# Attention outputs moved from a transpose bank to the two-bank ring, with eleven fillers fewer

## The chip, the cores and the metric

The kernel runs on one core of one Trainium2 chip. The metric is the device time of one execution in microseconds; lower is better. The time before is the median of three runs. The profile comes from one execution, whose own time stands beside its span.

## The reference

A gated block over `x` of 8 batches x 100 tokens x 512. First a cross-attention to a context of 8 x 361 x 256 (16 query heads, 8 key heads of 128), then a transformer layer whose self-attention and mixture of experts are what follows here:

```
h = rms(layernorm(x)) * w_ln1
q, k, v = h @ wq + bq, h @ wk + bk, h @ wv + bv      # 16 heads of 32
q, k = rope(q, k)
attn = softmax(causal(q k^T / sqrt(32)))             # 100 x 100 per head and batch
x = x + (attn @ v) @ wo
h = rms(x) * w_ln2;  top-2 of 8 experts (352 wide) + a shared expert (1408 wide)
```

All of it is in fp32 quality. The large products are done as three matmuls on a high and a low part of each operand (`mm3`).

## The kernel before, in words

Each engine runs its own list of instructions in order, and semaphores tie them together. One list of steps, `steps_ffn`, sets the order of the second half of the kernel for all engines; each engine picks its part out of each step.

The 8 batches are in two halves of 4. Self-attention is the step `("at", n)`, n from 0 to 35. A unit u (0 to 31) is four heads of one batch: batch u // 4. The four heads of a unit have one bank of scores (banks 0, 1, 2, 5) and one tile `PF`. The way of a unit goes over several steps:

- PE: `f_scores(q, pair)`, the scores of two units of batch q, two steps or more ahead ("scores q").
- DVE: `f_max`, the row extremum; ACT: four exponentials into `PF`; DVE: reciprocal, and the scaling multiplication (from unit 22 on POOL does the multiplication, L1993).
- PE at step u + 3: "turn u", four transposes of `PF` into bank 3 (even u) or bank 4 (odd u), L2413. ACT copies the even ones to `PTf`, DVE the odd ones (L1593).
- PE at step 4q + 7: "out q", `f_out(q)`, 16 small products of batch q, into bank 4 in the kernel before. ACT copies the bank to `CXh` (the high part, L1132), and DVE subtracts to get `CXl` (the low part, event `dve_cx`).

On ACT and DVE the work of step n is done in this order: the copy of the transposed unit, then CXh or CXl, then the exponentials (ACT), or the scaling and the next row extremum (DVE).

Between the steps stand other products of PE. They take two banks in turn, 6 and 7, which is called the ring here. `Plan.banks` walks through the list of steps and gives each user the next bank of the two and, as its wait, the event with which the previous user of that bank was emptied. `free_bank` waits for it. Users of the ring, in order: `qk` 0 to 7 of the second half (query and key products), `vbat` 0 to 3 (value products of the second half; DVE's addition `("vadd", i)` of the bias, L1574, empties the bank), `po` 0 to 3 (output projection), `er` 0 to 3, `eh` 0 to 3 (transposes, with DVE work on the rows between them), `elog`, `gate` 0, `esoft` (LT transposes, L2462), `up` 0, and the second half's `po`. In the list, `("at", 15)` (with out 2) stands between `vbat` 1 and `vbat` 2, and `("vadd", 1)` right behind `("at", 15)`. `("at", 35)` (with out 7) is followed by `esoft` 0 and `up` 0. After step `moe1` the ring has all eight banks.

Fillers are products of the identity with itself, whose results nobody reads (`keep_warm`). Each shows in the trace as two matmul records. `WARM` places some in front of named work. `WARM_RING` places others, and gives with the number the user of the ring in whose bank they are written; so a group of fillers also waits for that bank.

`mm` (L2074) is the helper that issues most matmuls, so this line stands for many kinds of work; the tiles tell them apart. L1357 is the same for DVE's subtractions (low parts).

Of the kernel before, what the change touches and what calls it, by code (L numbers as in the profile page):

```python
# [21 lines left out]
FH, FD = 16, 32  # L22
# [30 lines left out]
WARM = {"head": 12, ("x_turn", 0, 1): 3, ("q", 0, 0): 4, "swap": 4, "vrow": 7, "scores": 4, ("turn", 3): 2, ("po", 0, 0): 3,  # L53
        ("elog", 0): 3}

WARM_RING = {("scores", 2, 0): (4, ("qk", 1, 5)), ("turn", 9): (3, ("vbat", 0)), ("scores", 5, 0): (5, ("po", 0, 0)),
             ("turn", 21): (3, ("er", 0, 1)), ("scores", 7, 0): (2, ("er", 0, 3)), ("out", 5): (3, ("eh", 0, 0)),
             ("turn", 25): (6, ("eh", 0, 0)), ("out", 6): (3, ("eh", 0, 3)), ("turn", 29): (2, ("elog", 0)),
             ("out", 7): (4, ("esoft", 0))}

AHEAD = {"x": 3, "f": 4, "e": 4}
SLOTS = {"x": 4, "f": 6, "e": 6}
# [291 lines left out]
class Plan:  # L354
# [86 lines left out]
    def banks(self):  # L441

        empty = {6: ("dve_x1", 7), 7: ("dve_x1", 8)}
        self.bank, self.bank_free = {}, {}
        count, n, ring = {}, 0, [6, 7]

        def signal(name):
            count[name] = count.get(name, 0) + 1
            return name, count[name]

        def use(key, gone):
            nonlocal n
            bank = ring[n % len(ring)]
            self.bank[key], self.bank_free[key] = bank, empty[bank]
            empty[bank] = gone
            n += 1

        for s in self.ffn:
            if s[:2] == ("qk", 1):
                use(s, ("act_f", 8 - len(BY_PE) + s[2] + 1))  # L460
            elif s[0] == "vbat":
                use(s, ("dve_v", HB + s[1] + 1))
            elif s[0] == "po":
                use(s, ("act_ytf", s[1] * KD + s[2] + 1))
            elif s[0] == "er":
                use(s, ("dve_x2", s[1] * HB + s[2] + 1))
            elif s[0] == "eh":
                use(s, ("dve_h2", s[1] * HB + s[2] + 1))
            elif s[0] == "elog":
                use(s, ("act_lt", s[1] + 1))  # L470
            elif s[0] == "esoft":
                use(s, ("dve_l", s[1] + 1))
            elif s[0] == "moe1":
                empty |= {0: ("act_fe", 32), 1: ("act_fe", 32), 2: ("act_fe", 32), 5: ("act_fe", 32), 3: ("act_ft", 16), 4: ("dve_cx", 8)}
                n, ring = 0, list(range(8))
            elif s[0] == "gate":
                gone = signal("act_th")
                use(s, gone if s[2] else signal("dve_silu"))
            elif s[0] == "up":
                use(s, signal("dve_gu"))  # L480
            elif s[0] == "down" and s[3] == 0:
                use(s[:3], ("act_y", s[1] * KD + s[2] + 1))
            elif s[0] == "rank":
                use(s, ("dve_route", ROUTE["pos"]))
            elif s[0] == "inverse":
                use(s, ("dve_meta", 3))
            elif s[0] == "xt":
                use(s, ("dve_xe", s[1] + 1))
            elif s[0] == "eg":
                use(s, ("act_et", s[1] + 1))  # L490
            elif s[0] == "eu":
                use(s, ("dve_em", s[1] + 1))
            elif s[0] == "ea":
                use(s, ("dve_ea", s[1] + 1))
            elif s[0] == "ed":
                use(s, ("act_ey", s[1] + 1))
            elif s[0] == "srow":
                use(s, ("dve_sr", s[1] * HB + s[2] + 1))
# [15 lines left out]
def flamingo_kernel(nc, x, ctx_in, mask, g_x, g_f, Wq, Wk, Wv, Wo, w_ln1, wq, b_q, wk, b_k, wv, b_v, wo,  # L514
# [6 lines left out]
    def sem(name):  # L521
        if name not in handles:
            handles[name] = top.enter_context(nc.semaphore(name))
        return handles[name]
# [367 lines left out]
    def scalar_program(eng):  # L892
# [227 lines left out]
        def self_attention(n):  # L1120
            u = n - 3
            if 0 <= u < 32 and u % 2 == 0:
                act.wait_ge(sem("pe_ft"), u + 1)
                if u >= 6:
                    act.wait_ge(sem("pe_fo"), (u - 6) // 4 + 1)
                eng.activation(flat(PTf[u % 6][:, :, :]), banks[3 + u % 2][0:T, 0:4 * T], ACT.Copy).then_inc(sem("act_ft"), 1)
            u = n - 4
            if u >= 0 and u % 4 == 3:
                h, b = divmod(u // 4, HB)
                act.wait_ge(sem("pe_fo"), u // 4 + 1)  # L1130
                src = banks[4][:, 0:4 * T].rearrange("p (a b) -> p a b", a=4)
                eng.activation(CXh[h][:, :, batch_slice(b)], src, ACT.Copy).then_inc(sem("act_cx"), 1)  # L1132
            u = n
            if u < 32:
                act.wait_ge(sem("dve_fn"), u + 1)
                if u >= 4:
                    act.wait_ge(sem("pe_ft"), u - 3)
                p, m, bank = PF[u % 4], sm[u % 4], score_bank[u % 4]
                for c in range(4):
                    e = eng.activation(p[:, c, :], bank[0:T, c * T:(c + 1) * T], ACT.Exp, bias=m[:, 1, c:c + 1],  # L1140
                                       scale=-1.0, accum_out=m[:, 2, c:c + 1])
                e.then_inc(sem("act_fe"), 1)
# [199 lines left out]
    def vector_program(eng):  # L1342
# [242 lines left out]
        def self_attention(n):  # L1585
            if n == 0:
                f_max(0)
            u = n - 3
            if 0 <= u < 32 and u % 2:
                dve.wait_ge(sem("pe_ft"), u + 1)  # L1590
                if u >= 6:
                    dve.wait_ge(sem("pe_fo"), (u - 6) // 4 + 1)
                eng.tensor_copy(flat(PTf[u % 6][:, :, :]), banks[3 + u % 2][0:T, 0:4 * T]).then_inc(sem("dve_ft"), 1)  # L1593
            u = n - 4
            if u >= 0 and u % 4 == 3:
                h, b = divmod(u // 4, HB)
                dve.wait_ge(sem("act_cx"), u // 4 + 1)
                src = banks[4][:, 0:4 * T].rearrange("p (a b) -> p a b", a=4)
                low(CXl[h][:, :, batch_slice(b)], src, CXh[h][:, :, batch_slice(b)]).then_inc(sem("dve_cx"), 1)
            u = n - 1  # L1600
            if 0 <= u < 32:
                p, m = PF[u % 4], sm[u % 4]
                dve.wait_ge(sem("act_fe"), u + 1)
                if u in BY_POOL:
                    eng.reciprocal(m[:, 3, :], m[:, 2, :]).then_inc(sem("dve_frec"), 1)
                else:
                    chained(eng.reciprocal(m[:, 3, :], m[:, 2, :]))
                    r4 = m[:, 3, :].rearrange("p (a o) -> p a o", o=1).broadcast_to([T, 4, T])
                    eng.tensor_tensor(p[:, :, :], p[:, :, :], r4, ALU.mult).then_inc(sem("dve_fp"), 1)
            if n + 1 < 32:  # L1610
                f_max(n + 1)
# [457 lines left out]
    def tensor_program(eng):  # L2069
# [3 lines left out]
        def mm(o, a, b, start, stop):  # L2073
            return eng.matmul(o, a, b, start=start, stop=stop, skip_group_check=True)  # L2074
# [303 lines left out]
        def f_out(q):  # L2378

            h, b = divmod(q, HB)  # L2380
            warm_ring("out", q)
            pe.wait_ge(sem("act_ft"), 2 * q + 2)
            pe.wait_ge(sem("dve_ft"), 2 * q + 2)
            pe.wait_ge(sem("dve_v"), HB * (h + 1))
            if q:
                pe.wait_ge(sem("dve_cx"), q)
            else:
                pe.wait_ge(sem("dve_ht"), B - 1)
            for c in range(4):
                for i in range(4):  # L2390
                    at = (4 * c + i) * FD
                    e = mm(banks[4][32 * i:32 * i + 32, c * T:(c + 1) * T], V[h][:, b, at:at + FD],
                           PTf[(4 * q + i) % 6][:, c, :], True, True)
            e.then_inc(sem("pe_fo"), 1)

        def self_attention(n):
            u = n - 3
            if 0 <= u < 32:
                warm_ring("turn", u)
                if u < 2:  # L2400
                    pe.wait_ge(sem("dve_v"), HB)
                    pe.wait_ge(sem("dve_ht"), B - 1)
                elif u % 2 == 0:
                    pe.wait_ge(sem("act_ft"), u // 2)
                else:
                    pe.wait_ge(sem("dve_ft"), u // 2)
                    if u >= 5:
                        pe.wait_ge(sem("dve_cx"), (u - 5) // 4 + 1)
                keep_warm(banks[3 + u % 2], WARM.get(("turn", u), 0))
                name, value = plan.scaled(u)  # L2410
                pe.wait_ge(sem(name), value)
                for c in range(4):
                    e = eng.transpose(banks[3 + u % 2][0:T, c * T:(c + 1) * T], PF[u % 4][:, c, :], ident[0:T, 0:T])  # L2413
                e.then_inc(sem("pe_ft"), 1)
# [276 lines left out]
```

## Time and profile before

| | |
|---|---|
| median of 3 runs | 929.7 us (928.98 to 931.67) |
| profiled execution | 929.81 us, span 928.0 us |
| PE busy | 901.6 us (97%) |
| PE weight load busy | 842.2 us (91%) |
| DVE busy | 634.6 us (68%) |
| ACT busy | 559.1 us (60%) |
| POOL busy | 323.9 us (35%) |
| mean granted TensorE clock | 0.996 |
| chain that ended last | PE 61%, DVE 17%, DMA 12% |
| self-attention stage | about 507 to 617 us of the span |

Busy times are sums over the whole span. The chain is followed back from the last instruction, at each step to what released it. The self-attention stage is where the change is; its rows stand two sections below. A matmul row's time is that of a merged piece, start first, then duration.

### The profile page before, as it was taken

The page shows a single profiled execution, that of the slowest core. Times are in us where ns is not written, and L with a number is a line of the kernel's source. Part 1 is how long each engine was busy: PE and PEld are TensorE (multiplying, and loading weights), DVE is VectorE, ACT ScalarE, POOL GpSimd, SP SyncE. Part 2 cuts the span into 40 slices and gives each one's busy share as a digit, 9 for nine tenths or more (in the row PEclk, how much of TensorE's full clock was granted, in tenths as well). Part 3 has the DMA queues.
Part 4 walks back from the last instruction along what each step waited for, and adds up shares of the span by engine and source line. Part 5 has one row for each costly group of instructions (what it writes and reads, how often), then busy time and mean ns, then how long its engine had stood idle before and what let it go on. Part 6 is the DMA issues. An engine that isn't in the chain of part 4 may idle for free.

```text
span 928.0 us, 16511 instructions
## 1 busy us (share of the span) xinstructions
PE 901.6 (97%) x5905; PEld 842.2 (91%) x5905; DVE 634.6 (68%) x1482; ACT 559.1 (60%) x1448; POOL 323.9 (35%) x344
## 2 busy tenths in 40 slices
PE   8999999999999999999999999899999999999996
PEld 8889999999999999999987877689999999999996
DVE  3657777664446777673286985857585989898864
ACT  3666766663555666674432766745436787778851
POOL 3532323335552223234643542334401232323211
PEclk9999999999999999999999999999999999999999
DMA  5733720006450000002542111114438899999975
GB/s 158 217 93 109 202 82 2 7 18 173 141 160 23 17 1 1 2 12 58 157 117 85 58 51 54 48 59 116 115 93 291 291 328 319 332 303 328 298 193 153
DMA packets 112761, 122.22 MB, mean 132 GB/s; under 512 B 9887, under 2 KB 77927, under 8 KB 112680
## 3 DMA queue, kind: packets, MB, share of 16 engines
q1 hardware_dynamic: 97806, 98.80, 34.0%
q0 software_dynamic: 5184, 12.13, 5.8%
q10 hardware_dynamic: 9690, 10.24, 3.8%
q8 instruction: 47, 0.77, 0.3%
q14 instruction: 34, 0.28, 0.1%
HBM read 110.72 MB, written 19.07 MB: 140 GB/s over the span
## 4 chain that ended last, share of the span: by engine, by line
PE 61%; DVE 17%; DMA 12%; issue 4%; ACT 4%; POOL 1%; ACTq 0%; SPq 0%; DVEq 0%; POOLq 0%
PE bank L2074 55%; DMA eraw<-in_L_ffn_w_gate_e_dram 8%; PE bank L2223 4%; DVE we L1357 2%; DVE wf L1357 2%; ACT we L930 1%; DMA raw<-in_L_xattn_Wq_dram 1%; DMA sums<-s_sum 1%; DVE TE L1782 1%; DVE sm L1583 1%; DMA raw<-s_unit 1%; DMA X<-in_x_dram 1%; DVE HDl L1357 1%; DVE PQ L1559 1%; DVE TM L1767 1%
## 5 line engine op out<-in xcount | busy, mean ns | idle before, releaser
L1943 POOL TENSOR_SCALAR SC<-SC,mx,anyv 100x361 f32<-100x361 f32 x128 | 81.7, 650 | 210.1 <-DVE mx L1468 199.2
L1357 DVE TENSOR_TENSOR we<-eraw,we 128x704 fp32r<-128x704 f32 (+2 forms) x140 | 107.4, 798 | 25.2 <-ACT we L930 25.0
L930 ACT ACTIVATE we<-eraw 128x704 fp32r<-128x704 f32 (+2 forms) x140 | 96.7, 719 | 39.4 <-DMA eraw<-in_L_ffn_w_gate_e_dram 22.4
L1926 POOL TENSOR_TENSOR wx<-raw,wx 128x512 fp32r<-128x512 f32 x64 | 83.5, 1314 | 72.4 <-ACT wx L916 72.3
L1926 POOL TENSOR_TENSOR wf<-raw,wf 128x512 fp32r<-128x512 f32 x54 | 71.7, 1334 | 103.4 <-ACT wf L916 103.4
L2074 PE MATMUL bank<-H2h,wf 128*128 128x400 f32 x352 | 100.2, 351 | 0.0
L1046 ACT ACTIVATE SC<-SC,mx 100x361 f32<-100x361 f32 x128 | 75.4, 593 | 29.1 <-DVE mx L1464 28.3
L1357 DVE TENSOR_TENSOR Kl<-bank,Kh 128x362 fp32r<-128x362 f32 x64 | 34.0, 534 | 58.8 <-ACT Kh L1004 58.8
L1357 DVE TENSOR_TENSOR QOl<-bank,QOh 128x200 fp32r<-128x200 f32 (+1 forms) x96 | 41.4, 432 | 45.6 <-ACT QOh L959 35.5
L2074 PE MATMUL bank<-XTh,wx 128*128 128x400 f32 x256 | 70.8, 351 | 0.5 <-POOL wx L1926 0.5
L2004 POOL DMA_INDIRECT XB<-s_h,inv x20 | 22.2, 1108 | 140.5 <-PE bank L2520 116.8
L916 ACT ACTIVATE wf<-raw 128x512 fp32r<-128x512 f32 x100 | 61.6, 628 | 15.7 <-DMA raw<-s_unit 7.6
L2074 PE MATMUL bank<-QOh,wx 128*128 128x400 f32 x256 | 70.8, 347 | 0.0
L2074 PEld LDWEIGHTS bank<-H2h,wf 128*128 128x128 f32 x352 | 65.7, 189 | 0.1
L1461 DVE CUSTOM_DVE_ANT_0 SC<-bank,mb 100x361 f32<-100x361 f32 x128 | 62.6, 527 | 0.3
L1037 ACT ACTIVATE PTh<-bank 128x400 fp32r<-128x400 f32 x64 | 32.4, 506 | 50.1 <-PE bank L2223 49.9
L2074 PE MATMUL bank<-H2l,wf 128*128 128x400 f32 x176 | 60.7, 345 | 0.0
L1357 DVE TENSOR_TENSOR PTl<-bank,PTh 128x400 fp32r<-128x400 f32 (+1 forms) x128 | 53.2, 457 | 7.5 <-ACT PTh L1037 7.5
L916 ACT ACTIVATE wx<-raw 128x512 fp32r<-128x512 f32 x64 | 40.0, 627 | 26.7 <-PE bank L2074 8.9
L2074 PE MATMUL bank<-PTl,Vh 128*128 128x200 f32 (+1 forms) x192 | 52.8, 275 | 0.0
L2074 PE MATMUL bank<-PTh,Vl 128*128 128x200 f32 (+1 forms) x192 | 52.7, 275 | 0.0
L2074 PE MATMUL bank<-PTh,Vh 128*128 128x200 f32 (+1 forms) x192 | 52.0, 271 | 0.0
(291 smaller groups left out, 2730.6 us busy)
## 6 DMA issues: line engine op xcount, KB each, us to landing
raw<-s_unit SPq DMA_DIRECT2D x60, 256.0 KB, 3.1
eraw<-in_L_ffn_w_gate_e_dram SPq DMA_DIRECT2D x40, 352.0 KB, 4.5
eraw<-in_L_ffn_w_up_e_dram SPq DMA_DIRECT2D x40, 352.0 KB, 5.1
eraw<-in_L_ffn_w_down_e_dram SPq DMA_DIRECT2D x40, 256.0 KB, 5.4
raw<-in_L_xattn_Wq_dram SPq DMA_DIRECT2D x32, 256.0 KB, 3.2
raw<-in_L_xattn_Wo_dram SPq DMA_DIRECT2D x32, 256.0 KB, 2.9
eraw<-in_L_ffn_w_down_e_dram SPq DMA_DIRECT2D x20, 192.0 KB, 5.0
s_unit<-in_L_ffn_w_sh_gate_dram SPq DMA_DIRECT2D x11, 256.0 KB, 3.6
```

Source lines behind the costliest of these rows:

```text
L916: eng.activation(weights(stream, u)[:, 0, :, :], raw[r % 4][:, :, :], ACT.Copy).then_inc(sem("act_w"), 1)
L930: eng.activation(weights("e", u)[0:rows, 0, 0:n], eraw[u % 6][0:rows, 0:n], ACT.Copy).then_inc(sem("act_e"), 1)
L1037: eng.activation(flat(PTh[t % 2][:, 0:2, :]), banks[5][:, 0:4 * T], ACT.Copy).then_inc(sem("act_pt"), 1)
L1046: eng.activation(sc, sc, ACT.Exp, bias=mx[t % 3][:, 1, h:h + 1], scale=XS, accum_out=mx[t % 3][:, 2, h:h + 1]).then_inc(sem("act_exp"), 1)
L1357: return eng.tensor_tensor(o, src, f32(hi), ALU.subtract)
L1461: eng.tensor_tensor_reduce(SC[t % 3][:, h, :], banks[h][0:T, 0:S], mb[:, :], 1.0, -3.0e38, ALU.add, ALU.max, m[:, 0, h:h + 1]).then_inc(se ...
L1559: chained(eng.tensor_tensor(by_batch(p[:, 1, :]), by_batch(p[:, 1, :]), sin4, ALU.mult))
L1926: eng.tensor_tensor(w[:, 1, :, :], raw[plan.raw[stream, u] % 4][:, :, :], f32(w[:, 0, :, :]), ALU.subtract).then_inc(sem("pool_w"), 1)
L1943: eng.tensor_scalar(sc, sc, m[:, 3, h:h + 1], anyv[:, b:b + 1], ALU.mult, ALU.mult).then_inc(sem("pool_p"), 1)
L2004: eng.indirect_dma_start(XB[i % 2][:, :], None, s_h2, bass.IndirectOffsetOnAxis(ap=inv[:, i:i + 1], axis=0)).then_inc(sem(f"dma_xb{i % 2}" ...
L2074: return eng.matmul(o, a, b, start=start, stop=stop, skip_group_check=True)
L2223: e = eng.transpose(dst, SC[t % 3][:, h, o:o + n], ident[0:T, 0:T])
```

## The change

The outputs of self-attention become users of the ring: each takes the next of banks 6 and 7 when its step comes. ACT and DVE read them from there. PE's odd transposes lose their wait for `dve_cx`. The ring's later users move on by one place at every output. After `moe1`, bank 4 waits for the last copy of an odd transpose instead of for the last `CXl`. The filler groups before turn 9 (3), turn 21 (3) and turn 29 (2) go, that before turn 25 has 3 instead of 6, and the others are written into other users' banks.

```diff
--- before.py
+++ after.py
@@ -53,10 +53,8 @@
 WARM = {"head": 12, ("x_turn", 0, 1): 3, ("q", 0, 0): 4, "swap": 4, "vrow": 7, "scores": 4, ("turn", 3): 2, ("po", 0, 0): 3,
         ("elog", 0): 3}
 
-WARM_RING = {("scores", 2, 0): (4, ("qk", 1, 5)), ("turn", 9): (3, ("vbat", 0)), ("scores", 5, 0): (5, ("po", 0, 0)),
-             ("turn", 21): (3, ("er", 0, 1)), ("scores", 7, 0): (2, ("er", 0, 3)), ("out", 5): (3, ("eh", 0, 0)),
-             ("turn", 25): (6, ("eh", 0, 0)), ("out", 6): (3, ("eh", 0, 3)), ("turn", 29): (2, ("elog", 0)),
-             ("out", 7): (4, ("esoft", 0))}
+WARM_RING = {("scores", 2, 0): (4, ("out", 0)), ("scores", 5, 0): (5, ("out", 3)), ("scores", 7, 0): (2, ("er", 0, 3)),
+             ("out", 5): (3, ("out", 5)), ("turn", 25): (3, ("eh", 0, 0)), ("out", 6): (3, ("out", 6)), ("out", 7): (4, ("out", 7))}
 
 AHEAD = {"x": 3, "f": 4, "e": 4}
 SLOTS = {"x": 4, "f": 6, "e": 6}
@@ -460,6 +458,8 @@
                 use(s, ("act_f", 8 - len(BY_PE) + s[2] + 1))
             elif s[0] == "vbat":
                 use(s, ("dve_v", HB + s[1] + 1))
+            elif s[0] == "at" and s[1] >= 7 and s[1] % 4 == 3:
+                use(("out", s[1] // 4 - 1), ("dve_cx", s[1] // 4))
             elif s[0] == "po":
                 use(s, ("act_ytf", s[1] * KD + s[2] + 1))
             elif s[0] == "er":
@@ -471,7 +471,7 @@
             elif s[0] == "esoft":
                 use(s, ("dve_l", s[1] + 1))
             elif s[0] == "moe1":
-                empty |= {0: ("act_fe", 32), 1: ("act_fe", 32), 2: ("act_fe", 32), 5: ("act_fe", 32), 3: ("act_ft", 16), 4: ("dve_cx", 8)}
+                empty |= {0: ("act_fe", 32), 1: ("act_fe", 32), 2: ("act_fe", 32), 5: ("act_fe", 32), 3: ("act_ft", 16), 4: ("dve_ft", 16)}
                 n, ring = 0, list(range(8))
             elif s[0] == "gate":
                 gone = signal("act_th")
@@ -1128,7 +1128,7 @@
             if u >= 0 and u % 4 == 3:
                 h, b = divmod(u // 4, HB)
                 act.wait_ge(sem("pe_fo"), u // 4 + 1)
-                src = banks[4][:, 0:4 * T].rearrange("p (a b) -> p a b", a=4)
+                src = banks[plan.bank["out", u // 4]][:, 0:4 * T].rearrange("p (a b) -> p a b", a=4)
                 eng.activation(CXh[h][:, :, batch_slice(b)], src, ACT.Copy).then_inc(sem("act_cx"), 1)
             u = n
             if u < 32:
@@ -1595,7 +1595,7 @@
             if u >= 0 and u % 4 == 3:
                 h, b = divmod(u // 4, HB)
                 dve.wait_ge(sem("act_cx"), u // 4 + 1)
-                src = banks[4][:, 0:4 * T].rearrange("p (a b) -> p a b", a=4)
+                src = banks[plan.bank["out", u // 4]][:, 0:4 * T].rearrange("p (a b) -> p a b", a=4)
                 low(CXl[h][:, :, batch_slice(b)], src, CXh[h][:, :, batch_slice(b)]).then_inc(sem("dve_cx"), 1)
             u = n - 1
             if 0 <= u < 32:
@@ -2382,14 +2382,11 @@
             pe.wait_ge(sem("act_ft"), 2 * q + 2)
             pe.wait_ge(sem("dve_ft"), 2 * q + 2)
             pe.wait_ge(sem("dve_v"), HB * (h + 1))
-            if q:
-                pe.wait_ge(sem("dve_cx"), q)
-            else:
-                pe.wait_ge(sem("dve_ht"), B - 1)
+            bank = free_bank(("out", q))
             for c in range(4):
                 for i in range(4):
                     at = (4 * c + i) * FD
-                    e = mm(banks[4][32 * i:32 * i + 32, c * T:(c + 1) * T], V[h][:, b, at:at + FD],
+                    e = mm(bank[32 * i:32 * i + 32, c * T:(c + 1) * T], V[h][:, b, at:at + FD],
                            PTf[(4 * q + i) % 6][:, c, :], True, True)
             e.then_inc(sem("pe_fo"), 1)
 
@@ -2404,8 +2401,6 @@
                     pe.wait_ge(sem("act_ft"), u // 2)
                 else:
                     pe.wait_ge(sem("dve_ft"), u // 2)
-                    if u >= 5:
-                        pe.wait_ge(sem("dve_cx"), (u - 5) // 4 + 1)
                 keep_warm(banks[3 + u % 2], WARM.get(("turn", u), 0))
                 name, value = plan.scaled(u)
                 pe.wait_ge(sem(name), value)
```

## Rows read from the trace of the kernel before

**Rows 1.** Busy time of each engine in four stretches: busy (count) for each, clock, DMA share, GB/s.

```profile
511.00:550.90 39.90, 37.54 (x345) 31.77 (x343) 37.85 (x76) 29.60 (x130) 20.79 (x16) 1.00 0.18 54
550.90:584.80 33.90, 33.03 (x328) 27.09 (x329) 18.19 (x42) 21.43 (x93) 10.76 (x8) 1.00 0.21 62
584.80:604.50 19.70, 16.40 (x180) 12.92 (x182) 19.28 (x45) 14.71 (x74) 6.83 (x8) 0.97 0.12 36
604.50:617.00 12.50, 11.57 (x128) 10.15 (x128) 2.86 (x8) 5.85 (x16) 2.99 (x3) 0.91 0.12 39
```

**Rows 2.** The chain that ended last, around 550 us: start, us, what.

```profile
550.25 0.58 DVE KT L1562
550.87 4.37 PE bank L2074 x30
```

**Rows 3.** Who PE waited for, 660 to 928 us, longest: us, times, longest.

```profile
PE bank L2074 <- DVE we L1357: 1.1, 2, 0.6
```

**Rows 4.** Who PE waited for, 505 to 660 us.

```profile
PE bank L2413 <- DVE CXl L1357: 1.8, 3, 1.0
```

**Rows 5.** PE in order of time: start, us, instruction, [idle before]; turns 5, 6, fillers, turn 10.

```profile
534.09 0.55 PE L2413 MATMUL bank<-ident,PF 100*100 100x100 f32 x4 [1.04 <-DVE CXl L1357]
535.79 0.55 PE L2413 MATMUL bank<-ident,PF 100*100 100x100 f32 x4
544.27 0.83 PE L2074 MATMUL bank<-ident 128*128 128x128 f32 x6
547.17 0.55 PE L2413 MATMUL bank<-ident,PF 100*100 100x100 f32 x4
```

**Rows 6.** Two scalings on DVE, POOL beside the first, all 22 (ns min/median/max).

```profile
534.15 1.40 DVE L1609 TENSOR_TENSOR PF<-PF,sm 100x400 f32<-100x400 f32 x1
545.53 1.40 DVE L1609 TENSOR_TENSOR PF<-PF,sm 100x400 f32<-100x400 f32 x1
533.84 1.28 POOL L1926 TENSOR_TENSOR wf<-raw,wf 128x512 fp32r<-128x512 f32 x1 [2.96 <-ACT wf L916]
L1609 DVE TENSOR_TENSOR PF<-PF,sm x22: 574/574/1477, 511.3 to 580.1; 100x400 f32<-100x400 f32 x22
```

**Rows 7.** ACT and PE in order of time, around turn 21.

```profile
585.84 0.23 ACT L1140 ACTIVATION_READ_ACCUMULATOR PF<-bank,sm 100x1 f32 x1
586.12 0.54 PE L2074 MATMUL bank<-causb,identb 100*100 100x400 bf16 x2
```

**Rows 8.** PE and DVE around out 2 and vbat 2.

```profile
555.51 0.89 PE L2074 MATMUL bank<-PTf,V 100*32 100x100 f32 x32
556.34 0.71 PE L2074 MATMUL bank<-wf,HTh 128*100 128x512 f32 x2
557.01 0.57 DVE L1357 TENSOR_TENSOR CXl<-bank,CXh 128x400 fp32r<-128x400 f32 x1 [2.76 <-ACT CXh L1132]
558.68 0.68 DVE L1574 TENSOR_TENSOR V<-bank,bvb 100x512 f32<-100x512 f32 x1
```

**Rows 9.** DVE's CXl of out 3, and the product of PE that waited for it.

```profile
569.43 0.57 DVE L1357 TENSOR_TENSOR CXl<-bank,CXh 128x400 fp32r<-128x400 f32 x1 [2.08 <-ACT CXh L1132]
570.15 0.42 PE L2074 MATMUL bank<-CXh,wf 128*128 128x400 f32 x1 [0.46 <-DVE CXl L1357]
```

**Rows 10.** PE, ACT and DVE around up 0.

```profile
616.72 0.45 PE L2074 MATMUL bank<-H2h,wf 128*128 128x400 f32 x1
616.56 0.50 ACT L1132 ACTIVATE CXh<-bank 128x400 fp32r<-128x400 f32 x1 [1.90 <-PE bank L2074]
617.09 0.57 DVE L1357 TENSOR_TENSOR CXl<-bank,CXh 128x400 fp32r<-128x400 f32 x1 [1.63 <-ACT CXh L1132]
```

**Rows 11.** Stretches around 603 us, columns as in rows 1, and out 6 on PE.

```profile
600.00:603.00 3.00, 1.61 (x12) 1.07 (x12) 3.00 (x7) 2.94 (x18) 0.85 (x1) 1.00 0.46 135
603.40:603.60 0.20, 0.20 (x3) 0.20 (x2) 0.20 (x3) 0.20 (x1) 0.00 (x0) 0.50 0.35 133
604.43 1.56 PE L2074 MATMUL bank<-PTf,V 100*32 100x100 f32 x32
```

## The prediction

> **What bounds the kernel now.** I read the page first: PE is busy 97% of the span, and the chain that ended last is 61% PE. That average says nothing about the stretch which the change edits, so I read stage by stage. The table of stretches [rows 1] splits the self-attention stage (511 to 617 us) by engine. From 511.0 to 550.9 DVE is busy 37.85 of 39.9 us while PE, with its fillers, still leaves 2.4 us idle; from 584.8 to 604.5 DVE is busy 19.28 of 19.7 us and PE only 16.4. Between them, 550.9 to 584.8, PE is busy 33.03 of 33.9 and DVE 18.19. The chain of waits says the same: it runs on DVE up to the addition that ends the rotary embedding at 550.83, and goes over to PE at 550.87 [rows 2], where the scores of batch 4 wait for that addition. So there are two parts where DVE sets the pace and one between them where PE does. After 617 us PE is the pace again: its whole list of waits from 660 us on has three lines, the largest 1.1 us [rows 3]. A delay of PE that is not made good by 617 us therefore reaches the end, and so does a gain.
>
> **What the change removes.** It takes the attention outputs ("out q") off bank 4, so the odd transposes ("turn u") need not wait for the subtraction that reads that bank (CXl), and drops 11 fillers. Waits of PE's transposes for CXl: 1.8 us over three [rows 4]. Fillers: three took 0.83 us [rows 5], so 0.28 each, and 11 take 3.0 us. At most 4.8 us in all. How much lies on the path?
>
> Turn 5, 1.04 us idle before 534.09 [rows 5]. Without it PE does turn 5 and scores 2 about 1.0 us sooner, and then stands at turn 6. Turn 6 needs the scaling of its tile, a DVE multiplication that ran 534.15 to 535.55 [rows 6]; PE started turn 6 at 535.79 [rows 5]. So at most 0.2 us is left of the 1.04. The same at turn 9: 0.83 of fillers and 0.37 of waiting go, turn 10 needs a multiplication that ran 545.53 to 546.93 and started itself at 547.17 [rows 5, 6], again 0.2 left. The scores of batch 4 then wait for the addition at 550.83 whatever PE did before [rows 2], and DVE had no gap that PE could close. Gain of both: 0. Bounds: 0 and the 2.2 us that stood there.
>
> Turn 21 (three fillers): next comes the second half of scores 6, started at 586.12, which needs an exponential that ACT ended at 586.07 [rows 7]. ACT does it behind the copy of out 4. Gain 0, with PE idle there instead. Turn 25 (six fillers become three, and a wait of 0.40): PE comes to the next transposes of the router rows (eh) 0.2 to 0.4 us sooner, but turn 27 after those waits for POOL, which waits for DVE, full in this part [rows 1]. Gain 0. Turn 29 (two fillers): the router's product after it waits for the low part of the last H2 tile, which hangs on ACT's queue behind out 6. Gain 0. What is left of the edit is PE idle in place of fillers.
>
> Here the Trainium skill bears on the DVE parts. The trace shows the scaling multiplication of turn 6 at 1.40 us while POOL ran a product from 533.84 to 535.12, while the median of all 22 is 0.57 [rows 6]. GPSIMD Engine Reference, Specifications: GpSimd shares its SBUF interfaces with VectorE and collides with VectorE instructions that have two SBUF inputs. By that rule each pair that meets or parts is worth about 0.8 us either way on the DVE path, and the sum would be 0.8 more or less.
> By the rows no POOL product moves here, since each starts behind an ACT operation that starts behind DVE, and the term is 0.
>
> **What it adds.** "Out q" takes its turn in the ring of banks 6 and 7, so every later user of the ring moves by one place at each out. I went through the ring user by user: bank, the event that frees it, and when that event stood in this trace. Nearly all stay covered (the nearest are the products that now need the CXl of an out: qk 6 for out 0, where turn 5, which waited for that same CXl, stands 2 us before it; and in the same way vbat 0, er 1 and eh 1, each behind a turn that waited for that CXl). Two do not.
>
> *First stall: vbat 2.* The order is vbat 0 (bank 6), vbat 1 (bank 7), out 2 (bank 6), vbat 2 (bank 7). So vbat 2 now waits for the bias addition that empties vbat 1; before, for that of vbat 0, long done. On DVE this addition is queued behind step 15, and step 15 holds CXl of out 2, which waits for ACT's copy of out 2, which waits for PE's out 2: the product right before vbat 2. The trace has the whole chain: out 2 is over at 556.34 and vbat 2 starts at once; ACT copies; DVE's CXl, which had waited 2.76 us for that copy, starts at 557.01, then a reciprocal, a multiplication and a maximum, and the addition runs 558.68 to 559.36 [rows 8]. From a DVE end to PE's start is 0.15 us (570.00 to 570.15) [rows 9]. So vbat 2 starts at 559.51 and not 556.34: 3.17 us. This is in the PE part; behind it turn 13, scores, vbat 3, turns 14 and 15 follow on PE, and ACT's exponential that scores 5 waits for stands behind turn 14. All move. Bounds: 0, if the addition came earlier, and 3.2.
>
> *Second stall: up 0.* Near the end gate and up of the first hidden tile also use the ring. Up 0 had the bank of gate 0; now it has that of out 7, so it waits for the CXl of out 7. Between the two PE has only four small transposes. Up 0 started at 616.72; ACT's copy began at 616.56, and CXl ran 617.09 to 617.66 [rows 10]. With 0.15 for the release up 0 starts at 617.81: 1.09 us. The output product that comes after needs this CXl anyway, but PE did all of up 0 before it, so nothing makes this good. Bounds 0 and 1.1.
>
> **The clock.** The granted clock is 1.00 almost everywhere, but 0.50 around 603.4 to 606.6 (the 1.2 of the two levels, 1.2 and 2.4 GHz), after 600 to 603 in which PE was busy 1.61 of 3.0 us [rows 11]. The low stretch was about 3.4 us long, and PE's work in it took nearly twice: out 6 1.56 us, out 2 0.89 [rows 8, 11]. The first stall leaves PE without any work for 3.17 us, less than in that stretch, so I expect a low stretch there too, at a place where PE sets the pace. If all 3.4 us of it fall on work they cost 1.7 us; part will fall on the idle time itself. Bounds 0 and 1.7; I take 1.3, nearer to the upper, since the stall is followed by solid work. For the second stall (1.1 us) I take nothing: the 1.04 us of idle before turn 5 [rows 5] did not lower it.
>
> **Sum.** 3.17 + 1.09 + 1.3 - 0 = 5.56 us. The profiled execution took 929.81 us (span 928.0 and 1.8 around it), 0.1 above the median of 929.7. 929.81 + 5.56 = 935.4; against the median, 935.3.
>
> **Rivals.**
> *A: the clock holds at vbat 2.* The stall is one block between solid work, unlike the torn stretch of 600 to 603. For it: nothing else lowered the clock in the middle of this stage. Against: no other idle block of PE there is longer than 1.04 us. Then 929.8 + 4.26 = 934.0.
> *B: PE set the pace after all (other side).* If the DVE parts give way because PE feeds them sooner, the waits and fillers removed count in full: 929.8 - 4.8 + 4.3 = 929.3, not slower. It decides once more than 3 of the 4.8 us are on the path. For: PE is 97% busy. Against: DVE's 37.85 of 39.9 and 19.28 of 19.7 [rows 1], and the step at 550.87 [rows 2].
> *C: more low stretches.* Between 584.8 and 604.5 PE loses fillers that stood between gaps. One more low stretch on work costs up to 1.7: 937.0. The Trainium skill speaks for this one, TensorE: Matmul & The Clock Gate, "A second HAM failure mode: psum-queue depth-cycling": a PE that often idles a little between groups of matmuls can fall to the low clock over and over. Against: there the path is DVE's, and slow PE work is partly hidden.
> *D: the old low stretch misses out 6.* Out 6 took 1.56 against 0.89 for out 2 [rows 8, 11], and the fillers ahead of it lose about as much: 1.3 us in all. If the low stretch falls elsewhere: 935.3 - 1.3 = 934.0.
> *E: the change does not make vbat 2 wait* (DVE gets to the addition earlier than I read): 929.8 + 1.1 = 930.9.
>
> **Chances.** Forecast 0.47 (own range 934.4 to 936.5), A 0.20, C 0.12, D 0.09, B 0.08, E 0.04. The range reaches over A, D and C and leaves out B and E: 931.8 to 937.6. About 0.3%, 2.8 us, can be told from no change with this kernel, so "slower" begins at 932.5. B and E and the edge of A are within it: same 0.14; slower 0.83; faster 0.03.
>
> **What would show it.** After: PE idle about 3.2 us between out 2 and vbat 2, ended by DVE's addition to V; about 1.1 us between the LT transposes and up 0, ended by CXl; no wait of turn 5, 9 or 25 for CXl; turn 6 still behind DVE's multiplication; DVE as full as before up to the scores of batch 4, which start no more than 0.3 us from 550.9; a granted clock of 0.5 for a few us behind vbat 2's start. If batch 4's scores start 1 us or more sooner, B is right; if vbat 2 starts at once, the forecast is wrong at its main term.

## The result, and the profile after

The changed kernel takes 939.6 us (median of 6 runs, 935.5 to 942.5), against 930.2 us for the kernel before in the same runs. The ratio is 1.0089, 95% interval 1.0071 to 1.0107, so it is slower by 8.3 us (6.6 to 10.0). The forecast was 935.3 us with a range up to 937.6: the sign was right, the size too small. A second set of six runs gave 938.8 us and a ratio of 1.0096 (1.0070 to 1.0122). The mean of all 12 is 939.1; that of all 104 executions of the kernel before in this study is 930.6, with single executions between 926.1 and 934.4.

The profiled execution is the longest of its six, 942.45 us. These are four lines of its page: the span, PE's busy time, the granted clock in 40 slices, and the chain that ended last.

```profile
span 940.6 us, 16466 instructions
...
PE 903.9 (96%) x5883; PEld 842.5 (90%) x5883; DVE 633.9 (67%) x1482; ACT 559.5 (59%) x1448; POOL 322.2 (34%) x344
...
PEclk8999999999999999999999999989999999999999
...
PE 64%; DVE 16%; DMA 10%; ACT 4%; issue 4%; POOL 1%; ACTq 0%; SPq 0%; DVEq 0%; POOLq 0%
```

PE is busy 2.3 us more than before in a span that is 12.6 longer; the clock shows an 8 in two slices where before had none (the first of them at the start of the kernel, in code that did not change). Whom PE waited for, 505 to 660 us (us in total, times, longest), answers to [rows 4]:

```profile
PE bank L2074 <- DVE V L1574: 3.0, 1, 3.0
PE bank L2074 <- ACT PF L1140: 2.8, 5, 1.0
PE bank L2408 <- POOL PF L1993: 2.0, 3, 1.0
PE bank L2408 <- DVE PF L1609: 1.9, 2, 1.0
PE bank L2074 <- DVE CXl L1357: 1.5, 2, 1.0
```

The waits of the transposes for CXl, 1.8 us before, are gone. In their place stand two waits of transposes for DVE's scaling (DVE PF), one of vbat 2 for the bias addition (DVE V), and one of up 0 for CXl, 1.0 of the 1.5 us in the last row; the other 0.5 stood before too [rows 9].

**First stall.** PE, then DVE, around out 2 and vbat 2, to be held against [rows 8]:

```profile
559.86 0.89 PE L2074 MATMUL bank<-PTf,V 100*32 100x100 f32 x32
563.76 0.76 PE L2074 MATMUL bank<-wf,HTh 128*100 128x512 f32 x2 [3.01 <-DVE V L1574]
...
564.75 1.05 PE L2074 MATMUL bank<-wf,HTh 128*100 128x512 f32 x2
565.60 0.63 PE L2074 MATMUL bank<-wf,HTl 128*100 128x512 f32 x1
...
567.95 0.40 PE L2074 MATMUL bank<-wf,HTl 128*100 128x512 f32 x1
```

```profile
561.36 0.57 DVE L1357 TENSOR_TENSOR CXl<-bank,CXh 128x400 fp32r<-128x400 f32 x1 [2.76 <-ACT CXh L1132]
...
563.03 0.68 DVE L1574 TENSOR_TENSOR V<-bank,bvb 100x512 f32<-100x512 f32 x1
```

Out 2 ends about 560.7, and vbat 2 starts at 563.76, 0.05 us behind the end of the addition at 563.71. Before, it followed out 2 at once. The columns below are as in [rows 1]; the clock is the third number from the end.

```profile
562.00:563.00 1.00, 0.00 (x0) 0.00 (x0) 0.97 (x3) 0.63 (x4) 0.00 (x0) 1.00 0.12 33
564.00:565.00 1.00, 1.00 (x4) 0.71 (x4) 0.00 (x0) 0.56 (x4) 0.00 (x0) 0.63 0.00 0
568.00:569.00 1.00, 1.00 (x10) 0.59 (x8) 0.27 (x1) 0.00 (x0) 0.00 (x0) 1.00 0.00 0
610.00:612.00 2.00, 1.08 (x8) 0.72 (x8) 2.00 (x5) 1.81 (x10) 0.85 (x1) 1.00 0.40 113
612.00:619.00 7.00, 6.86 (x55) 5.83 (x56) 3.34 (x10) 2.97 (x12) 1.95 (x3) 0.51 0.15 47
```

After the 3.01 us without any PE work (562 to 563 is one of them) the clock is low from about 564.3 on, for 3.4 us; in 568 to 569 it is back. While it is low one pair of matmuls of vbat 2 takes 1.05 us instead of 0.62. It falls a second time, after 610 to 612 where PE was busy 1.08 of 2 us, and stays low for almost 7 us, about twice as long as before [rows 11]. In a second trace of the changed kernel (experiment 5) that second fall lasted 3.4 us, as before.

**Second stall.** PE, then DVE, around up 0, to be held against [rows 10]:

```profile
625.97 0.36 PE L2457 MATMUL bank<-ident,LT 10*100 10x10 f32 x4
627.35 0.42 PE L2074 MATMUL bank<-H2h,wf 128*128 128x400 f32 x1 [1.02 <-DVE CXl L1357]
```

```profile
626.63 0.57 DVE L1357 TENSOR_TENSOR CXl<-bank,CXh 128x400 fp32r<-128x400 f32 x1 [1.63 <-ACT CXh L1132]
```

**Where waits went.** Turns 5 and 6 on PE and DVE's CXl and scaling, to be held against [rows 5, 6]:

```profile
537.25 0.51 PE L2408 MATMUL bank<-ident,PF 100*100 100x100 f32 x4
...
540.04 0.52 PE L2408 MATMUL bank<-ident,PF 100*100 100x100 f32 x4 [0.96 <-DVE PF L1609]
```

```profile
537.83 0.57 DVE L1357 TENSOR_TENSOR CXl<-bank,CXh 128x400 fp32r<-128x400 f32 x1
...
538.51 1.38 DVE L1609 TENSOR_TENSOR PF<-PF,sm 100x400 f32<-100x400 f32 x1
```

Turn 5 starts at 537.25, ahead of CXl (537.83), so its wait is gone. Turn 6 then stands 0.96 us for the scaling that ends at 539.89. The chain of waits around the scores of batch 4 answers to [rows 2], and goes over from DVE's addition to PE in the same way:

```profile
554.59 0.58 DVE KT L1562
555.18 0.04 issue
555.22 4.36 PE bank L2074 x30
```

To compare kernels I took the starts of seven products of PE in each trace and the time between them. Such a table leaves out what chance does elsewhere. "sc" is a first product of scores, "er" the first transposes of the second half (628.50 us before); the stages are sc 0 to sc 4; sc 4 (first pair) to sc 4 (second pair), with vbat 1 and 2 and out 2 in it; from there to out 4; out 4 to out 7; out 7 to er; er to the end of the span. All us, worked out from the timelines.

```
run                 start   sc4    vbat2   out4   out7    er     end
before             507.56  43.31   8.65   23.77  32.32  12.89  299.50
changed            510.36  44.86  13.31   23.80  32.81  13.96  301.50
changed, again     508.22  43.31  13.31   23.78  32.48  13.96  300.64
1  addition moved  508.49  43.32   8.64   23.78  33.46  13.96  300.25
2  no stall        506.21  44.85   8.64   23.78  33.50  12.90  299.82
3  stall filled    507.66  43.32  11.74   23.77  32.50  13.96  300.65
4  11 fillers back 508.02  43.32  13.32   23.77  33.00  13.96  301.41
6  before, -11     507.84  43.30   8.63   23.78  33.90  12.89  303.36
7  2 and 4         508.98  43.32   8.65   23.78  32.49  12.89  299.49
8  7, +5 fillers   507.19  43.30   8.64   23.79  31.10  12.90  301.08
9  clock held      508.30  43.30  11.74   23.77  31.11  13.88  299.80
10 out 7 back      506.63  43.29  13.28   23.81  32.50  12.90  301.09
11 before, +5      508.10  43.55   8.65   23.77  31.11  12.89  299.83
12 delay at vbat2  508.62  43.58  11.82   23.78  32.50  12.89  301.81
13 delay at 619    507.96  43.32   8.63   23.78  32.27  16.02  299.02
14 9, 2nd alone    508.16  43.33   8.63   23.79  31.13  13.90  299.56
15 9, 1st alone    506.44  43.29  11.76   23.77  31.11  12.90  300.23
```

(The fifth experiment is "changed, again"; a number in a name stands for the kernel of that experiment.) Stages that no edit touches repeat to 0.05 us where the clock is the same. The two 44.85 are executions in which the clock was low for 3.4 us between 509 and 517, in code that every kernel has; in the first 5 us of this stage the chain that ended last is on PE (5.14 us from 507.56 on, before), and there a slow clock costs time. In 11 and 12 it was low at 536 to 540, where DVE sets the pace, and cost 0.25. The start and the last column vary by 4 us between executions. In the first trace 2.8 us were lost before 507 us, 1.55 at 513 and 2.0 behind er. The three stages in between that the change touches cost 4.66 + 0.49 + 1.07 = 6.2 of its 12.6 us.

### The profile page after: what moved, and what is told of

Its sections match the earlier page's. It is cut to its first block, busy times and chain, and to the rows that moved or that the text cites. A ratio compares the mean times of both kernels' runs of the same rounds, so it can differ in the third digit from the quotient of the medians.

```text
span 940.6 us, 16466 instructions
## 1 busy us (share of the span) xinstructions
PE 903.9 (96%) x5883; PEld 842.5 (90%) x5883; DVE 633.9 (67%) x1482; ACT 559.5 (59%) x1448; POOL 322.2 (34%) x344
## 4 chain that ended last, share of the span: by engine, by line
PE 64%; DVE 16%; DMA 10%; ACT 4%; issue 4%; POOL 1%; ACTq 0%; SPq 0%; DVEq 0%; POOLq 0%
PE bank L2074 58%; DMA eraw<-in_L_ffn_w_gate_e_dram 5%; PE bank L2223 4%; DVE we L1357 2%; DMA raw<-in_L_xattn_Wo_dram 1%; DVE wf L1357 1%; ACT we L930 1%; DVE sm L1583 1%; DMA raw<-in_L_xattn_Wq_dram 1%; POOL wx L1926 1%; DMA sums<-s_sum 1%; DMA eraw<-in_L_ffn_w_down_e_dram 1%; DVE PQ L1559 1%; DMA raw<-s_unit 1%; DMA X<-in_x_dram 1%
```

## The experiments

Theories: 1, the two new stalls and the low clock they bring; 2, only their length, the rest being chance or a cost elsewhere (in the expectations of 5 and 9: some other cost of 2 us or more); 3, the missing fillers; 4, later, a delay of PE that costs more than its length.

**1. First stall taken away.**

```diff
-[("vadd", 0), ("vbat", 1), fetch], [("vadd", 1), ("vbat", 2)]
+[("vadd", 0), ("vbat", 1), ("vadd", 1), fetch], [("vbat", 2)]
```

> The changed kernel with DVE's bias addition for vbat 1 one place earlier in the list, ahead of step 15, so vbat 2 finds its bank free. Theory 1 (the two new stalls, 3.2 and 1.1 us, cost their length, and the low clock that they bring costs the rest): the 3.0 us idle before vbat 2 is gone, and the low stretch behind it too; 4.7 us less than the changed kernel, about 934.5. Theory 2 (only the stalls' length comes from the change; the rest of the 9.4 us is low clock that falls anywhere in the kernel by chance): 3.2 us less, about 936.4, with the mean granted clock as low as in the changed kernel (0.987 to 0.991). Theory 3 (the eleven fillers that went cost most of it): the clock stays low between 590 and 620 us, about 936.

932.2 us, ratio 1.0009 (0.9993 to 1.0024): by the ratios 7.4 us less than the changed kernel. PE in its trace:

```profile
556.45 0.89 PE L2074 MATMUL bank<-PTf,V 100*32 100x100 f32 x32
557.27 0.71 PE L2074 MATMUL bank<-wf,HTh 128*100 128x512 f32 x2
```

Vbat 2 follows out 2 at once. The step around it is back to 8.64, and the second stall is untouched (13.96). So this one wait carries most of the loss, and more than even theory 1 gave it. Not all of it: the interval reaches 2.2 us above the kernel before, and the stages of this trace are 2.2 above (1.1 at the second stall, 1.1 between out 4 and out 7).

**2. Both stalls taken away.**

```diff
-            elif s[0] == "at" and s[1] >= 7 and s[1] % 4 == 3:
+            elif s[0] == "at" and 7 <= s[1] < 35 and s[1] % 4 == 3:
...
-            bank = free_bank(("out", q))
+            bank = free_bank(("out", q)) if q < 7 else banks[4]
```

with the edit of 1, and ACT and DVE reading out 7 from bank 4.

> The changed kernel with the addition moved as in the first, and with out 7 back on bank 4, so that up 0 has the bank of gate 0 again: both new stalls gone, the other outs still in the ring, no waits of turns for CXl, eleven fillers fewer. Theory 1: as the kernel before, 929 to 931, since DVE sets the pace where waits and fillers went. If PE set the pace there, 925 to 927. Theory 2: 5 us of low clock remain, 934 to 935. Theory 3: 933 to 935, with more low clock than before between 584 and 620 us.

931.1 us, 1.0007 (0.9990 to 1.0025): as before. All waits of turns for CXl are gone here and eleven fillers too, and nothing is gained. That fits the reading that DVE, not PE, sets the pace there. Out 4 to out 7 is 1.2 us longer, with the clock low for 10 us from 601.

**3. The first stall filled.**

```diff
+            if i == 2:
+                keep_warm(banks[4], 12)
             bank = free_bank(("vbat", i))
```

> The changed kernel with twelve fillers (2.8 us) in bank 4 right before vbat 2 waits: the stall keeps its length, but PE is busy in it. It prices the clock's part of the first stall alone. Theory 1: no low stretch behind vbat 2, 1.3 to 1.7 us less than the changed kernel, about 938. Theory 2: no difference, 939 to 940.

935.8 us, 1.0064 (1.0042 to 1.0085). PE and the stretch behind it:

```profile
556.46 2.94 PE L2074 MATMUL bank<-ident 128*128 128x128 f32 x24
559.54 0.71 PE L2074 MATMUL bank<-wf,HTh 128*100 128x512 f32 x2
```

```profile
559.00:563.00 4.00, 3.87 (x22) 2.70 (x20) 0.56 (x2) 1.33 (x8) 0.00 (x0) 1.00 0.00 0
```

Clock 1.00 behind the stall. The step takes 11.74 instead of 13.31: the stall's length is 3.09 us and its low clock 1.57. The time fell by 2.3 us by the ratios (the forecast for theory 1 was 1.3 to 1.7), which the intervals allow.

**4. The eleven fillers back** (before turns 9, 21, 25 and 29, in the odd transposes' bank).

> The changed kernel with the eleven fillers back at their places (3 before turn 9, 3 before turn 21, 3 more before turn 25, 2 before turn 29), written into the bank of the odd transposes, which waits for nothing new. Theory 1: the stalls remain; at most 1 us less than the changed kernel, 938.5 to 939.6. Theory 3: 3 to 5 us less, 935 to 936.5.

937.3 us, 1.0057 (1.0032 to 1.0082). It lies between what theories 1 and 3 expected. By the ratios it is 3.0 us less than the changed kernel, which theory 3 would give, but the intervals overlap (3.0 to 7.6 us above before, against 6.6 to 10.0), and no stage of its trace is shorter. This run does not decide.

**5. The changed kernel again.**

> The changed kernel once more, as it is, to part the change's cost from chance. By landmarks, the first run of it cost 4.7 us around vbat 2, 1.1 before up 0, 0.5 between out 4 and out 7: 6.2 in all. Theory 1 (these three are the whole cost, the rest of the first 9.4 us was low clock at places that the change does not touch): 936 to 938 beside a kernel before of 931, and the same three differences by landmarks. Theory 2 (something else in the changed kernel adds 2 us or more in every run): 939 to 940 again.

938.8 us, 1.0096. The stages cost 4.66 + 0.16 + 1.07 = 5.9 us, as in the first trace but for out 4 to out 7, and the time is 8.9 above before by the ratio, 8.2 by the medians. Some 2 to 3 us are missing, so theory 2's outcome, and not theory 1's, came.

**6. The kernel before without the eleven fillers.**

> The kernel before with only the eleven fillers gone, banks and waits as they were. If bare waits in place of fillers lengthen the low clock around 603 us: out 4 to out 7 takes 1 to 1.2 us longer than before (the two kernels without either stall and without fillers took 33.5 us for it, before 32.3), 932. If fillers cost nothing either way: 931.

932.0 us, 1.0020 (1.0001 to 1.0038). Stretches of its trace, columns as in [rows 1]:

```profile
598.00:603.00 5.00, 4.67 (x32) 3.60 (x28) 5.00 (x11) 4.18 (x23) 1.71 (x2) 0.55 0.28 84
603.00:607.00 4.00, 3.93 (x44) 3.18 (x42) 1.76 (x5) 1.46 (x6) 0.85 (x1) 0.50 0.17 51
607.00:612.00 5.00, 4.63 (x19) 3.70 (x18) 1.80 (x5) 1.71 (x10) 1.70 (x2) 0.50 0.14 41
```

The clock is low for nearly 14 us, and out 4 to out 7 takes 33.90 instead of 32.32. So the missing fillers cost about 1.9 us here (0.1 to 3.5). The low stretch around 600 us took 3.4 to 13.7 us in the seven traces without the eleven fillers, and 3.4 or 6.8 in the five that have them and no others: a tendency, with one trace a kernel. No run shows that the fillers are more than a small part of the loss: 7 below, which has them, is not faster than 2, which lacks them.

**7. Both stalls gone, fillers back.**

> Both new stalls gone and the eleven fillers back in the odd transposes' bank, outs 0 to 6 still in the ring, no turn waiting for CXl. DVE sets the pace (first scores to scores 4 took 43.3 us in four kernels of five): as the kernel before within 0.5 us, 930.5 to 931.5, out 4 to out 7 in 32.3 to 32.5. If PE set the pace: 927 to 929.

932.2 us, 1.0025 (1.0009 to 1.0042), with stages as before to 0.2 us. The stages came as the expectation had them; the median lies 0.7 us above it. Nothing is gained by the freed waits here either. By the ratio the kernel is 2.3 us slower than before (0.8 to 3.9), and its stages explain 0.2 of it: time is missing here too, in a kernel without a stall.

**8. As 7, with fillers in the waits that lower the clock.**

```diff
-("turn", 25): 3, ("turn", 29): 2,
+("turn", 25): 3, ("turn", 27): 3, ("turn", 28): 2, ("turn", 29): 2,
```

> As the third, with three fillers more before turn 27 and two more before turn 28, where PE stands idle 0.9 and 0.5 us. If the idle time of 599 to 603 us is what lowers the clock there, the low stretch goes: out 4 to out 7 in 31.0 to 31.5 us, 1 us less than the kernel before, 929.5 to 930. If not, as the third.

928.35 us, 0.9978 (0.9964 to 0.9993): 2.0 us faster than the kernel before. Two stretches and two pieces of PE, against [rows 11]:

```profile
600.00:603.00 3.00, 2.03 (x16) 1.52 (x15) 3.00 (x7) 2.80 (x15) 0.85 (x1) 1.00 0.44 124
603.00:607.00 4.00, 3.60 (x56) 3.01 (x54) 2.06 (x7) 2.54 (x11) 1.71 (x2) 1.00 0.20 62
```

```profile
602.68 0.94 PE L2074 MATMUL bank<-ident 128*128 128x128 f32 x6 [0.48 <-DVE H2l L1357]
603.54 0.89 PE L2074 MATMUL bank<-PTf,V 100*32 100x100 f32 x32
```

PE is busy 2.03 of 3.0 us before 603, where it was 1.61; the clock stays at 1.00, and out 6 takes 0.89 us instead of 1.56. The stage is 1.2 us shorter than before. None of the five traces with these five fillers (8, 9, 11, 14, 15) has a low stretch there; each of the twelve others has one. Against 7 the stage is 1.4 us shorter and the time 4.4 by the ratios: again more than the stages show.

**9. The changed kernel, both stalls left, the clock held**: edits of 3, 4 and 8, and four fillers before up 0.

> The changed kernel with both stalls left at their length, and PE kept busy wherever it newly stands idle: 12 fillers before vbat 2, 4 before up 0, the eleven that went, and the five more before turns 27 and 28 of the eighth run. It prices the stalls' length alone, with the low clock taken out. The eighth run was 2.1 us under the kernel before. Theory 1 (stalls 3.1 and 1.1 us, the rest of the 8.4 us is low clock): 4.2 above the eighth, 2.1 above before: 932.5 to 933. Theory 2 (some other cost of 2 us in the changed kernel): 934.5 or more.

935.5 us, 1.0047 (1.0030 to 1.0064), mean clock of its ten runs 0.997. By stages it is 2.9 us above before, by time 4.4, and the interval (2.8 to 6.0) just reaches the stages. Against 8, whose twelve runs have the same mean clock, the stages are 4.1 longer and the time 6.4, with both intervals together about 4.3 to 8.5. So it is unlikely that the missing time is low clock.

**10. Only the second stall taken away.**

> The changed kernel with only out 7 back on bank 4: the second stall goes, the first stays. out 7 to the half's first er transposes takes 12.89 us instead of 13.96. Theory 1: 1.1 to 1.5 us less than the changed kernel's 939, 937.6. If the second stall also lowered the clock in part of the executions: 936 to 937.

937.6 us, 1.0060 (1.0041 to 1.0080), mean 936.5. The second stall is 1.07 us in the table (12.89 before against 13.96). By the ratios the kernel is 2.7 us faster than the changed one, with intervals that overlap (3.8 to 7.5 us above before, against 6.6 to 10.0).

**11. The kernel before with the five fillers of 8.**

> The kernel before with three fillers before turn 27 and two before turn 28, nothing else. If the low clock around 603 us is all that the eighth run gained by: out 4 to out 7 in 31.1 us instead of 32.3, 928.5 to 929.5, the same as the eighth, and the ring change is worth nothing even without its two stalls. If the freed waits helped the eighth: 930 or more.

929.7 us, 0.9984 (0.9968 to 1.0000). Out 4 to out 7 is 31.11, as in 8. The intervals of 8 and 11 overlap: the gain of 8 is the clock's, as far as can be told, and the ring change adds nothing that shows.

**12 and 13. A plain delay in the kernel before**: fourteen fillers before vbat 2, or before the second half's first output product.

```diff
             bank = free_bank(("vbat", i))
+            if i == 2:
+                keep_warm(bank, 14)
```

> The kernel before with fourteen fillers (some 3.3 us of PE work) ahead of vbat 2, nothing else. If a delay there costs its length: 3.2 us above before, 934. If it costs more later (theory 4: the expert stage's transfers fall worse behind a later start): 5 to 6 above before, 936 to 937, and the excess lies behind 640 us.

> The kernel before with the same fourteen fillers ahead of the second half's first output product, at 619 us. Its length alone: 3.3 above before, 934. Theory 4, if it holds for any delay before the expert stage: 5 to 6 above, as the one at vbat 2. Both differ if only the self-attention stage makes it worse.

935.9 us, 1.0057 (1.0038 to 1.0076), and 934.9 us, 1.0056 (1.0034 to 1.0077). The delay in the twelfth:

```profile
557.67 3.39 PE L2074 MATMUL bank<-ident 128*128 128x128 f32 x28
560.82 0.71 PE L2074 MATMUL bank<-wf,HTh 128*100 128x512 f32 x2
```

The stage grew by 3.17 us in one and by 3.13 in the other; the times by 5.3 and 5.2. No bank and no wait was changed. In the twelfth the mean clock of the six runs is that of the kernel before in the same set (0.994 and 0.995). That speaks for theory 4, at either place, though the lower ends of the intervals (3.5 and 3.2 us) lie only just above the length. Its second half, that the excess lies behind 640 us, is not shown: the last column is 301.81 in one and 299.02 in the other.

**14 and 15. One stall each, clock held.**

> The changed kernel with the clock held by the same fillers as in e9_held, the addition moved (first stall gone), the second stall left. Its length alone: 1.0 above e8_keep's 2.1 below before, so 929.7. If the missing 2.5 us belong to the second stall: 932.

> The changed kernel with the clock held, out 7 back on bank 4 (second stall gone), the first stall left. Its length alone: 3.1 above e8_keep, 1.0 above before, 931.7. If the missing 2.5 us belong to the first stall or to a delay there: 934.2.

930.2 us, 1.0000 (0.9980 to 1.0020), and 933.0 us, 1.0035 (1.0020 to 1.0050). Against 8, by the ratios, the second stall costs 2.0 us, the first 5.3, both together (9) 6.4; their lengths are 1.0, 3.1 and 4.1. For the first the interval of the cost, about 3.3 to 7.3, begins just above the length; for the second the length alone is well within it. Which of the two holds the missing part cannot be told.

## Why the prediction was right and where it fell short

**The mechanism** was right. Both stalls are where the walk through the ring put them: 3.17 forecast and 3.09 measured (experiment 3), 1.09 and 1.07 (experiment 10). The first was 0.08 shorter in part because vbat 2 started 0.05 us behind the addition and not 0.15. Experiment 1 shows that the first carries most of the loss. Rival E is out.

**Gain of the removed waits and fillers, 0**: right. The stage to the scores of batch 4 is 43.3 us in all kernels but for low clock by chance, with and without the waits and fillers; turn 6 waits for the scaling as foreseen. That scaling took 1.38 us again, beside a product of POOL, and not 0.57. Before and after, the same five scalings of the 22 took 1.38 to 1.48 us, so among them no pair of DVE and POOL met or parted. The Trainium skill (GPSIMD Engine Reference, Specifications) names the contention: GpSimd's SBUF interfaces are shared with VectorE, and instructions of VectorE with two SBUF inputs, as this one, collide with it. The trace agrees; it changed nothing here. Rival B is out. At turn 21, PE idles and scores 6 wait for ACT:

```profile
595.15 0.54 PE L2074 MATMUL bank<-causb,identb 100*100 100x400 bf16 x2 [1.01 <-ACT PF L1140]
```

**Clock at vbat 2, 1.3**: 1.57 measured; the term was a little too small. Rival A is out: the clock fell in all four traces with this block of idle time.

**The 0 for what comes between out 4 and out 7** was slightly low: 0.2 to 0.5 us in the traces of the changed kernel, 1.6 where only the fillers went (experiment 6). Rival C was real but small. Rival D did not come: out 6 took 1.56 us again. Work of PE in short pieces with idle time between them went with a low clock in all twelve traces that have it around 600 us, and with none in the five in which two of the waits were filled; 1.2 us came back there (8). The Trainium skill (TensorE: Matmul & The Clock Gate, "A second HAM failure mode: psum-queue depth-cycling") says that a PE which often idles briefly between groups of matmuls goes back and forth between the two clock levels. The traces agree in that the clock fell behind short idle times, with PE busy 1.61 of 3.0 us [rows 11].

**The step that failed** is the one in the first part: "a delay of PE that is not made good by 617 us therefore reaches the end", which I used one for one, with no term for anything behind it. The stages add up to 4.66 + 0.2 to 0.5 + 1.07 = 5.9 to 6.2 us, near the forecast of 5.56, but the kernel is 8.3 to 8.9 slower: 2 to 3 us stand in none of the stages. Plain delays of 3.2 and 3.1 us cost 5.3 and 5.2 (12 and 13). In nine kernels with a delay of 3 us or more (changed twice, 3, 4, 9, 10, 12, 13, 15) the time, by its ratio, lies on average 1.5 us above the sum of the stages, the low clock near 513 left out; in the seven others 0.1 below. The single ones scatter widely: from -1.1 to 3.0 with a delay, from -1.4 to 2.1 without (the 2.1 is experiment 7), and their own intervals are 1.4 to 2.5 us either way. So the runs speak for an excess of some 1.5 us that goes with a long delay before the expert stage, with or without the ring change; they do not prove it.

The median lies 4.4 us above the forecast. Of these, 0.5 is that the kernel before had 930.2 us in the same runs and not 929.7; 1.1 is scatter between the medians' difference (9.4) and that of the ratio (8.3); 0.7 is terms of the sum that were too small (the clock at vbat 2, and the 0 between out 4 and out 7); 2.0 is the part of the step that failed. I had no term for the draw of runs.

**What stays open**: the cause of the excess, and where it lies. If the other executions have the stages of the traced ones, it is behind 640 us, where the expert stage's weights stream in, but the traces do not show it: er to the end takes 299.0 to 303.4 us in them, 300.7 on average with a delay and 300.4 without one. From er to PE's first product with expert weights it is 82.2 us in 15 of the 17 traces, so what varies lies mostly behind about 711 us. A trace per kernel is too few for 1.5 us in a stage that varies by 4.

## What to carry to other kernels

When a buffer ring gets one more kind of user, list for each later user the event that now frees its buffer and where that event's instruction stands in its own engine's queue. The product in the bank of vbat 1 was ready early, but the instruction that empties it stood behind one that waited for the product just issued; moving it one place took 7.4 of 8.3 us away (by the ratios of experiment 1 and the changed kernel). Removing waits from an engine that waits for another anyway gave nothing, and taking out the fillers that stood there cost about 1.9 us (0.1 to 3.5, experiment 6). Where an engine's time is made of repeating stages, compare them by landmarks; the single total here scattered by 7 us.

## What the runs showed of the hardware

- The clock fell once behind a block of 3.0 us without PE work (changed kernel twice, and 4 and 10), for 3.4 us each time; where the block was filled it did not, and the stage was 1.57 us shorter (3). It fell too behind 3.0 us in which PE was busy 1.61 in short pieces [rows 11], and not where fillers made it 2.03 (8).
- Low stretches of 3.4, 7, 10 and 14 us were seen at the same work around 600 us in different kernels. In code that was equal to that of other kernels without them, low stretches came at 509 to 517 us (two traces) or 536 to 540 (two). One of 3.4 us cost 1.55 us where PE's work was on the path, and 0.25 where DVE set the pace.
- Twelve products of a 128x128 identity, 24 matmul records, took 2.94 us, and the clock stayed at 1.00 behind them (3).
